# Layer 0's edge gather moved beside three other stages, as rows already multiplied by the weights

## The reference, cut to what matters

```
xn = layernorm(x)
# graph part of layer 0
xw = xn @ weight                                    # 12500 x 256
msgs = xw[src] * edge_weight[:, None]               # 200000 x 256
z = segment_sum(msgs, dst, num_segments=12500) + bias
# mixer of layer 0
qkv = xn @ Wqkv;  k = softmax(k, over the nodes);  context = k^T v (per head)
out = (q @ context) * sigmoid(gelu(layernorm(xn) @ Wg1 + bg1) @ Wg2 + bg2) @ Wproj + bproj
x = x + z + out
x = x + ffn0(layernorm(x))
# layer 1: a graph part with attention, a mixer, a selective feed-forward part
```

## Time and profile before

| what | us |
|---|---|
| median of 2 runs | 11478.49 (11473.49 and 11483.5) |
| the profiled execution | 11486.09, its span 11483.0 |
| `norm0` | 145 to 261 of the span |
| `aggregate0` | 261 to 2509, 2248 |
| `key_max` | 2509 to 2639.7, 131 |
| `context0` | 2639.7 to 2871.3, 232 |
| `mix0` | 2871.3 to 3409.1, 538 |

### The profile page before, as it was taken

How to read it: one execution, slowest core, us unless ns; L and a number is a source line. 1 busy time by engine, 2 the same in 40 slices (tenths; PEclk the granted TensorE clock), 3 DMA queues, 4 the chain that set the end, 5 groups by cost and what they waited for, 6 DMA issues and landing times. The chain is left out here.

```text
span 11483.0 us, 139138 instructions
## 1 busy us (share of the span) xinstructions
PE 8203.0 (71%) x31420; PEld 5820.8 (51%) x31421; DVE 4741.1 (41%) x15039; ACT 1390.6 (12%) x3054; POOL 5311.9 (46%) x5986
## 2 busy tenths in 40 slices
PE   2667777779878987648888820057778777787798
PEld 1444444445557766326666610035555555546687
DVE  4444444431122232325555512166666666544100
ACT  1000000002432222102222200000000000001121
POOL 2777777630000001767777764446676666502000
PEclk7777787789877988878889865589998999855899
DMA  5333333322001017111111100176666677632001
GB/s 186 102 101 102 102 102 98 89 82 68 28 19 62 21 40 211 33 35 20 21 19 21 20 16 23 32 221 186 190 196 200 205 209 212 187 91 75 22 18 57
DMA packets 568905, 1068.90 MB, mean 93 GB/s; under 512 B 161007, under 2 KB 295402, under 8 KB 568155
## 3 DMA queue, kind: packets, MB, share of 16 engines
q0 software_dynamic: 283600, 692.27, 22.0%
q1 hardware_dynamic: 252316, 328.10, 9.3%
q10 hardware_dynamic: 32927, 47.77, 1.2%
HBM read 894.49 MB, written 175.61 MB: 93 GB/s over the span
## 5 line engine op out<-in xcount | busy, mean ns | idle before, releaser
L1870 POOL DMA_INDIRECT agg_rows<-node_rows,agg_stage x1660 | 1623.1, 978 | 746.2 <-issue 354.8
L621 POOL DMA_INDIRECT agg_rows<-xn_rows,agg_stage x1660 | 1574.3, 948 | 593.5 <-issue 452.0
L681 PE MATMUL agg_ps_sum<-agg_rows,agg_sel_w 128*128 128x257 f32 x3320 | 1270.6, 519 | 506.4 <-DVE agg_sel L646 413.5
L1920 PE MATMUL agg_ps_g<-agg_rows,agg_sel_w 128*128 128x256 f32 x3320 | 1138.9, 427 | 456.8 <-DVE agg_att L1901 257.0
L2174 POOL DMA_INDIRECT mix_lots<-src_terms,mix_idx_stage x1196 | 1161.4, 971 | 390.1 <-issue 348.8
L645 DVE TENSOR_SCALAR agg_sel_w<-iota,dst_item,w_item 128x128 f32<-128x128 f32 x1660 | 759.2, 457 | 1213.7 <-DMA agg_rows<-xn_rows,agg_stage 1160.8
L681 PEld LDWEIGHTS agg_ps_sum<-agg_rows,agg_sel_w 128*128 128x128 f32 x3320 | 644.0, 241 | 844.5 <-issue 763.2
L1921 PE MATMUL agg_ps_a<-agg_att,agg_sel 128*128 128x260 f32 x3320 | 1069.3, 406 | 0.0
L1901 DVE TENSOR_TENSOR agg_att<-agg_rows,ee_item 128x256 f32<-128x256 f32 x1660 | 705.5, 425 | 787.8 <-DMA agg_rows<-node_rows,agg_stage 775.9
L1920 PEld LDWEIGHTS agg_ps_g<-agg_rows,agg_sel_w 128*128 128x128 f32 x3320 | 620.4, 204 | 807.3 <-issue 402.3
L1921 PEld LDWEIGHTS agg_ps_a<-agg_att,agg_sel 128*128 128x128 f32 x3320 | 679.8, 205 | 108.2
(11 more groups left out here) (463 smaller groups left out, 12865.0 us busy)
## 6 DMA issues: line engine op xcount, KB each, us to landing
xn_turned<-norm_xt SPq DMA_DIRECT2D x200, 256.0 KB, 2.7
agg_rows<-xn_rows,agg_stage POOLq DMA_INDIRECT x1660, 2.8
agg_rows<-node_rows,agg_stage POOLq DMA_INDIRECT x1660, 3.7
xn_rows<-norm_xn SPq DMA_DIRECT2D x100, 256.0 KB, 3.0
ctx_xt<-xn_turned SPq DMA_DIRECT2D x100, 256.0 KB
mix_xt<-xn_turned SPq DMA_DIRECT2D x100, 256.0 KB
ffn_xt<-xn_turned SPq DMA_DIRECT2D x100, 256.0 KB
node_rows<-tab_rows POOLq DMA_DIRECT2D x50, 512.0 KB, 3.2
```

What stands on the lines that cost most here:

```text
L621: pool.indirect_dma_start(rows[:, u, 0:C], None, g.xn_rows, bass.IndirectOffsetOnAxis(stage[:, half, u:u + 1], 0)).then_inc(landed[u], 16)
L681: pe.matmul(ps_sum[:, to], sel_w[:, u, :], rows[:, u, :], start=False, stop=False, skip_group_check=True)
L1870: pool.indirect_dma_start(rows[:, u, :], None, g.node_rows, bass.IndirectOffsetOnAxis(stage[:, u:u + 1], 0)).then_inc(landed[u], 16)
L1920: pe.matmul(ps_g[:, to], sel_w[:, u, :], rows[:, u, 0:C], start=False, stop=False, skip_group_check=True)
```

## The change

- `norm0` no longer stores the normalized rows. It multiplies each group by `L0_gnn_weight` as it goes (PE, four products of 256 columns), ACT copies these to `pr`, and SP stores them as rows of 258 floats to `h_rows`: 256 features and two ones.
- The items are put in 166 lots of 10. `EdgeRows` on POOL gathers a lot of `h_rows` into a ring of three lots, and stores it to DRAM (`edge_rows`, 128 partitions by 10,320 bytes). The phases `key_max`, `context0` and `mix0` stand ahead of the sum now, and POOL gathers lots 0 to 8, 9 to 25 and 26 to 65 in them; lots 66 to 165 are gathered in the new `aggregate0`.
- `aggregate0` on SP loads the lots back one after the other into two buffers, with 20 control words each (`ctl_row`: the PSUM bank, 0 or 512, and one more than the block's number). DVE makes the matrices of a whole lot with two operations. PE has no branches: for each five items it loads ten registers, waits with a register until the block's bank is free, and multiplies into the bank at a register's offset.
- ACT puts a block's x into the PSUM bank ahead of the block, waits for the count of the block's last item (`blk_end`), and copies the sum back to x. There is no transposition, product or bias any more; the bias is added to `bproj` in `mix0`.
- `item_code` is loaded in layer 1's `aggregate1` now.

The core of the diff:

```diff
@@ normalize
+                def keep_rows(gi, u, stored):
+                    act.wait_ge(projected, gi + 1)
+                    act.wait_ge(p_out[u], stored)
+                    act.activation(pr[:, u, :, 0:C], ps_p[bank_of[u]][:, :, :], ACT.Copy).then_inc(p_kept, 1)
...
+                def rows_product(gi, u, early):
+                    pe.wait_ge(kept, gi + 1)
+                    if not early:
+                        pe.wait_ge(p_kept, gi - 1)
+                    for j in range(GROUP):
+                        for c in range(KC):
+                            mm = pe.matmul(ps_p[bank_of[u]][:, j, :], xt[:, u, c, j * P:(j + 1) * P], pw_sb[:, c, :], start=(c == 0), stop=(c == KC - 1))
+                    mm.then_inc(projected, 1)
...
+                def store_product(gi, u):
+                    sp.wait_ge(p_kept, gi + 1)
+                    sp.dma_start(pw_rows[bass.ds(gi * ROWS, ROWS), :].rearrange("(j p) c -> p j c", p=P), pr[:, u, :, :]).then_inc(p_out[u], 16)
@@ the lots
+class EdgeRows:
...
+    def store(self, pool, g, lot):
+        s, turn = lot % LOT_RING, lot // LOT_RING
+        pool.wait_ge(self.landed[s], 16 * LOT_ROWS * (turn + 1))
+        pool.dma_start(g.edge_rows[lot, :, :], self.ring[:, s, :, :].rearrange("p i c -> p (i c)")).then_inc(self.stored[s], 16)
+    def run(self, pool, g, begin, end):
+        for lot in range(begin, end):
+            s, turn = lot % LOT_RING, lot // LOT_RING
+            if turn:
+                pool.wait_ge(self.stored[s], 16 * turn)
+            for i in range(LOT_ROWS):
+                item = lot * LOT_ROWS + i
+                pool.indirect_dma_start(self.ring[:, s, i, :], None, self.table,
+                                        bass.IndirectOffsetOnAxis(g.src_idx[:, item:item + 1], 0)).then_inc(self.landed[s], 16)
+            if lot:
+                self.store(pool, g, lot - 1)
@@ aggregate0
+                def load(lot, s, turn, early):
+                    sp.wait_ge(edges.stored[s % LOT_RING], 16 * turn + 16)
+                    if not early:
+                        sp.wait_ge(item_used, lot * LOT_ROWS - LOT_ROWS)
+                    sp.dma_start(rows[:, s % 2, :, :].rearrange("p i c -> p (i c)"),
+                                 g.edge_rows[bass.ds(lot, 1), :, :].rearrange("o p c -> (o p) c")).then_inc(loaded[s % 2], 16)
+                    sp.dma_start(ctl[:, s % 2, :], ...).then_inc(loaded[s % 2], 16)
...
+                        dve.tensor_tensor(sel[:, u, :, :], places, dst, ALU.is_equal).then_inc(eq_done, 1)
+                        dve.wait_ge(eq_done, lot + 1)
+                        dve.tensor_tensor(sel_w[:, u, :, :], sel[:, u, :, :], w, ALU.mult).then_inc(sel_ready, 1)
...
+                            _, v = nc.values_load_multi_w_load_instructions(
+                                ctl[0:1, u, 2 * at:2 * at + 2 * BATCH], [mybir.EngineType.PE], min_val=0, max_val=512, ...)
+                            for j in range(BATCH):
+                                off, need = v[2 * j], v[2 * j + 1]
+                                pe.wait_ge(free, need)
+                                pe.matmul(ps[:, bass.ds(off, W)], sel_w[:, u, at + j, :], rows[:, u, at + j, 0:W], start=False, stop=False, skip_group_check=True)
+                                pe.matmul(ps[:, bass.ds(off + W, 1)], sel[:, u, at + j, :], g.ones_bf[:, 0:1],
+                                          start=False, stop=False, skip_group_check=True).then_inc(item_used, 1)
...
+                def seed(b, u):
+                    act.activation(ps[:, u * BANK:u * BANK + C], x_block(g, b), ACT.Copy)
+                    act.activation(ps[:, u * BANK + C:u * BANK + W + 1], g.zeros2[:, :], ACT.Copy).then_inc(free, 1)
+                def keep(b, u):
+                    end = act.value_load(g.blk_end[0:1, bass.ds(b, 1)], min_val=1, max_val=ITEMS)
+                    act.wait_ge(item_used, end)
...
+        key_max(nc, g, lambda pool: edges.run(pool, g, 0, 9))
+        context0(nc, g, lambda pool: edges.run(pool, g, 9, 26))
+        mix0(nc, g, lambda pool: edges.run(pool, g, 26, 66))
+        aggregate0(nc, g, edges, 66)
@@ layer0_steps
-        lambda: normalize(nc, g, "norm0", g.xn_rows, g.xn_turned, second=g.rstd2),
-        lambda: aggregate0(nc, g),
-        lambda: key_max(nc, g),
-        lambda: context0(nc, g),
-        lambda: mix0(nc, g),
+        lambda: normalize(nc, g, "norm0", None, g.xn_turned, second=g.rstd2, project=(g.given["L0_gnn_weight"], g.h_rows)),
+        lambda: gather0(nc, g),
```

More of the change, by code:

```diff
@@ L550, in body @@
                             few(SLOTS * k + u - 1, (u - 1) % SLOTS)
+                        if project is not None and not (first and u == 0):
+                            rows_product(SLOTS * k + u - 1, (u - 1) % SLOTS, first and u <= 2)
                 peeled(pe, GROUPS // SLOTS, body)
@@ new lines, with __init__ @@
+class EdgeRows:
+    def __init__(self, ph, table):
+        self.table = table
+        self.landed = [ph.sem(f"landed{u}") for u in range(LOT_RING)]
+        self.stored = [ph.sem(f"stored{u}") for u in range(LOT_RING)]
+        self.ring = ph.sb("ring", [P, LOT_RING, LOT_ROWS, ROW])
+    def store(self, pool, g, lot):
[13 more added lines that the diff above has]
+                self.store(pool, g, lot - 1)
+        if end == LOTS:
+            self.store(pool, g, LOTS - 1)
+            for lot in range(LOTS - LOT_RING, LOTS):
+                pool.wait_ge(self.stored[lot % LOT_RING], 16 * (lot // LOT_RING + 1))
@@ new lines, in aggregate0 @@
+def aggregate0(nc, g, edges, begin):
+    BANK = 512
+    W = C + 1
+    with phase(nc, "agg0") as ph:
+        loaded = [ph.sem("loaded0"), ph.sem("loaded1")]
+        opened, kept, free, begun = (ph.sem(s) for s in ("opened", "kept", "free", "begun"))
+        eq_done, sel_ready, item_used = ph.sem("eq_done"), ph.sem("sel_ready"), ph.sem("item_used")
+        rows = ph.sb("rows", [P, 2, LOT_ROWS, ROW])
+        sel = ph.sb("sel", [P, 2, LOT_ROWS, P], BF16)
+        sel_w = ph.sb("sel_w", [P, 2, LOT_ROWS, P])
+        ctl = ph.sb("ctl", [1, 2, LOT_ROWS * 2], I32)
+        ps = ph.psum("sum", [P, 2 * BANK])
+        TURNS = LOTS // (2 * LOT_RING)
@@ L649, in _ @@
+                peeled(dve, LOTS // 2, body)
             @block.tensor
             def _(pe):
[L651 to L664 removed]
@@ L723, in _ @@
[L723 to L730 removed]
+                for u in range(2):
+                    mm = pe.matmul(ps[:, u * BANK:u * BANK + W + 1], g.zrow_bf[0:1, 0:P], g.zrow_bf[0:1, 0:W + 1], start=True, stop=True)
@@ new lines, in _ @@
+                mm.then_inc(opened, 1)
+                def body(k, first):
+                    for u in range(2):
+                        lot = 2 * k + u
+                        pe.wait_ge(loaded[u], 32 * k + 32)
+                        pe.wait_ge(sel_ready, lot + 1)
+                        pe.sem_inc(begun, 1)
+                        for at in range(0, LOT_ROWS, BATCH):
+                            _, v = nc.values_load_multi_w_load_instructions(
+                                ctl[0:1, u, 2 * at:2 * at + 2 * BATCH], [mybir.EngineType.PE], min_val=0, max_val=512,
+                                skip_runtime_bounds_check_because="item_tables writes 0 or 512, and one more than a block's number")
+                            for j in range(BATCH):
[4 more added lines that the diff above has]
+                                          start=False, stop=False, skip_group_check=True).then_inc(item_used, 1)
@@ new lines, in _, with gather0 @@
+                seed(0, 0)
+                seed(1, 1)
+                with act.Fori(0, NODE_BLOCKS // 2 - 1) as k:
+                    for u in range(2):
+                        keep(2 * k + u, u)
+                        seed(2 * k + u + 2, u)
+                for u in range(2):
+                    keep(NODE_BLOCKS - 2 + u, u)
+def gather0(nc, g):
+    with phase(nc, "rows0") as ph:
+        edges = EdgeRows(ph, g.h_rows)
+        key_max(nc, g, lambda pool: edges.run(pool, g, 0, 9))
+        context0(nc, g, lambda pool: edges.run(pool, g, 9, 26))
+        mix0(nc, g, lambda pool: edges.run(pool, g, 26, 66))
+        aggregate0(nc, g, edges, 66)
@@ L787, in key_max, with _ @@
         with nc.Block() as block:
+            @block.gpsimd
+            def _(pool):
+                fetch(pool)
             @block.sync
@@ L831, in _, with context0 @@
                 dve.tensor_copy(g.k_shift[:, :], ps_row[:, :])
-def context0(nc, g):
+def context0(nc, g, fetch):
     with phase(nc, "ctx0") as ph:
@@ L947, in _, with mix0 @@
                 peeled(act, PAIRS, body)
-def mix0(nc, g):
+def mix0(nc, g, fetch):
     H = C // 4
```

250 lines of the change are left out of this document (92 added, 158 removed).

## The result

The changed kernel took 10882.74 us (median of 2 runs, 10873.14 and 10892.33) against 11478.49 before: ratio 0.9481, 95% interval 0.944 to 0.9522. The forecast was 10820, its range 10,680 to 11,150. The profiled execution took 10873.14 us with a span of 10871.1, so 612 us less than the span of before. All of it, but some 14 us in layer 1, comes from the stages up to the new `aggregate0`.

The account below looks back on a forecast made before the run. Old `aggregate0` was taken as bound by POOL's gather issue, then PE's block changes; the new one by DMA. 11486.1 -2248 +1480 +50 +30 +8 +15 +5 gave 10826, so a median of 10820; range 10,680 to 11,150 us.

Parts of the forecast that it names:

- first rival: New `aggregate0`: PE sets the phase, 2.0 to 3.0 us of each register load uncovered, 1560 to 1890 us; chance 0.22.
- the sum's 10826: Whole kernel: the profiled 11486.1 us less 660 us, from the old and new `aggregate0` and the other stages' terms.
- the small terms: Outside `aggregate0`: `norm0` +50, `key_max` +30, `context0` +8, `mix0` +15 and other small things +5 us.
- PE's lot: New `aggregate0`: matmuls about 7.0 us plus two register loads showing 0.5 each, 8.0 us; 166 lots 1330 us.
- the DMA's 1480: New `aggregate0`: gathers 463 us plus stores and loads 1017 us keep all 16 DMA engines busy for 1480 us.
- POOL's lot: POOL's ten gathers of 1.25 us and a store of 0.95: 13.45 us; 100 lots in `aggregate0` 1345 us.
- 564 us in all, beside the rest: `aggregate0`: DVE's two operations per lot take 3.4 us, 564 us in all, running beside the other engines' work.
- The store in the middle: POOL's direct store per lot, queued ahead of the next lot's gathers: 0.95 us with its gap, no wait.
- fourth rival: POOL's gathers get dearer beside a busy DVE, at worst 1.48 us each, 16 a lot; chance 0.14 with the second rival.
- second rival: DMA engines hold up POOL's ring: 16 us a lot, phase 1600, whole 11,048 us; chance 0.14 with the fourth rival.
- The third, the slower one: `aggregate0`: PE at half clock with register loads in the open, 14.1 us a lot, whole 11,687 us; chance 0.05.
- 12.9: `aggregate0`: the time per lot in us from which the change loses, (2248 - 108) / 166.

Follow-up runs that it names:

- the second execution: The changed kernel run again, unaltered, in a later set on a chip where before takes 11,467 us: 10864.33 us, ratio 0.9476.
- the words hoisted: Against the changed kernel, a lot's 20 control words are loaded ahead of its rows, with their own semaphore: 10808.56 us, ratio 0.9429.
- the thinned loads: Against the changed kernel, SP loads back one of a lot's ten items from the third lot on (sum not computed): 10778.11 us, ratio 0.9392.
- six words: Against the changed kernel, PE loads six registers per five items, not ten; on a chip where before takes 13,821 us: 14283.7 us, ratio 1.0336.

## Why the prediction was right, and where it was off

**The sign and the source of the gain were right, what sets the end of the new phase was not.** The gathers are hidden in three stages at little cost, and `aggregate0` falls by 30%. But the forecast had the 16 DMA engines set its end, with PE waiting for `agg_rows<-edge_rows`. PE set it, idle on "issue", which the prediction had named as the sign of its first rival. The time lies in the range because the two mechanisms are only 80 us apart at the rival's lower end, and that is luck. The median is 63 us over the forecast; the profiled execution is 47 over the sum's 10826, which is 85 more in the phase, 22 less in the small terms and some 14 less in layer 1, which the sum didn't have.

**The step that was mis-sized is PE's lot.** "I take 0.5 us shown per load. A lot is then 8.0 us ... under the DMA's 1480." The matmuls' 7.0 us are right: 9.57 us a lot between 1300 and 2600 us in the second execution, less the two gaps of 1.66 and 0.90, leave 7.0. The gaps are 2.6 us and not 1.0. The first has to do with the load's place as well as its length: PE reads the words only when 1.32 MB of rows have landed, about 7 us behind their issue, in place of the 2.7 to 4.3 of the earlier trace rows, and with the words loaded first it fell by 0.4. Of the second load most does hide, as forecast: 0.90 us show of 2.41. Of the first nothing does. The first rival named 2.0 to 3.0 us uncovered for each load, at full clock. What came is 1.3 us for each, with matmuls at a clock of 0.85, so its 1560 us for the phase came out by two errors that cancel. It should have had more than 0.22.

**The DMA's 1480 us was no bound that was reached.** 485 MB in 1565 us are 310 GB/s. With the words hoisted it was 323 at a phase of 1503. That is close to the sum (1480 at 328), so the number was good as a floor, though it wasn't what set the end. The transfers act through the landing time: with nine tenths of the loads gone PE's lot fell to 7.8 us. The prediction's own range is not quite the sum of its bounds either: the lower ones add up to 10,650 against the profiled execution, not 10,680. Nothing hung on it.

**POOL's lot was put at 13.45 us.** In `mix0` it was 13.1 (stores of lots 32 and 64 at 814.3 and 1234.7 us), 3 us under the forecast for each ten lots, which is why `mix0` cost nothing. In `aggregate0` it was 14.6: ten gathers at 1.10 instead of 0.95, for the reason shown above. That is the fourth rival's mechanism, at a smaller price than its 1.48. The step "564 us in all, beside the rest" for DVE holds for DVE's own time (496 us), but it wasn't free: its 3.0 us a lot cost POOL 1.5. The store in the middle (0.95 forecast, 585 ns and a gap) was right, and its wait nothing.

**The small terms.** `norm0` +39 for +50: PE's product, at a clock of 0.99, lay better beside the transpositions than 120 us (its busy time is 110 in all). `key_max` +37 for +30: 24 us more of the wait forecast, and 18 us more of PE's busy time at the lower clock, which the sum didn't have. `context0` +6 for +8. The second rival (ring held by the DMA engines) is dead: 3.4 us of wait in the phase. The third, the slower one, was asked about half clock with the loads in the open, and the clock was 0.86. On the chips where PE is held the phase took 14 us a lot and more, over its 12.9, and every kernel with the change's gathers was slower than before. But 12.9 comes from the phase of before on the first chip, and no trace of before was taken on the others, so this is no test of it. The prediction had no word for a difference between chips: it holds for the kind of chip of the first comparison.

## What to carry to other kernels

When a lot's control words and its data share a semaphore, the register loads stand behind the landing: load the words first and wait for them apart (56 us here). When DVE work is batched into long operations with two SBUF inputs beside POOL's gathers, count their length against each gather that starts inside. One input in SBUF is no guarantee (L2541), but short operations cost little: with those of 128 columns no gather took over 1.08 us. And before a sum takes one resource as the bound, compare all that are within a tenth of it: here PE 1562, DMA 1480 (an estimate) and POOL 1470 us lay so close that removing 56 us from the first met the third.

## What the runs showed of the hardware that was not expected

- A load of registers from SBUF on PE's queue is not linear: one register 0.30 us, five 1.23, ten 1.08 or 2.40, the same instruction twice a lot, by its place (a lot's first or second half). Why the first ten are faster than five is open.
- The same load takes up to 6.5 us at times. In the kernel with the thinned loads, between 1300 and 2600 us, all 25 of a lot's first loads with packets of POOL's stores (10,320 bytes) in flight took over 1.2 us, and none of the 124 with none in flight did. In the unaltered change, where SP's loads move such packets too, it is less clear-cut: 21 of the 66 with POOL's packets in flight were not long. From 2715 us on, where POOL is silent, all take 1.08 or 2.41.
- A gather that starts inside a DVE operation with two SBUF inputs ends 0.82 us behind its end (250 of 887 in the unaltered change). A direct store from POOL is not held (40 that started inside, 0.585 us in the mean), nor is a DVE operation that starts inside a gather. A tensor-scalar operation with one SBUF input held the gathers too (23 of 23 inside L2541), a reciprocal of 3.35 us didn't (0 of 131).
- On two chips the same kernel before takes 13,800 us in place of 11,470, and every version tried of the change was slower than before there. With six words PE took 36 us a lot on one of them while POOL gathered, and 6.8 behind the last gather. A gain that rests on gathers beside PE's work should be timed on more than one chip.
